# A fused two-layer gated block in fp32 on one core: key and value projections issued between the steps of the first attention, first transfers in another order, an additive mask table, weight signs in other slices

## The reference, cut to what matters

```python
x = x + tanh(g_xattn[0]) * L0_xattn(layernorm(x), ctx, mask_b)   # stage A, one head, keys = values = ctx
x = x + tanh(g_ffn[0])   * L0_ffn(layernorm(x), w1, w2, w3)      # stage B
x = x + tanh(g_xattn[1]) * L1_xattn(layernorm(x), ctx, mask_i, Wq, Wk, Wv, Wo, ...)  # stage C, 16 heads
x = x + tanh(g_ffn[1])   * L1_ffn(layernorm(x), w_gate, w_up, w_down)  # stage D
```

## Time and profile before

| | us |
|---|---|
| median of 3 executions | 259.05 |
| lowest, highest | 258.74, 261.1 |
| the profiled execution: its time | 261.3 |
| the profiled execution: its span | 259.5 |
| stage A, about | 11 to 40 |
| stage B, about | 40 to 127 |
| stage C, about | 127 to 184 |
| stage D, about | 184 to 259.5 |

### The profile page before, as it was taken

The page is one execution under the profiler, slowest core; times in us unless marked ns, Lnnn a source line. Parts: engine busy times, 40 slices in busy tenths (PEclk is TensorE's granted clock), DMA queues, the critical chain, the costliest instruction groups (busy, mean ns, idle before and its releaser), DMA issues. The chain is left out here.

```text
span 259.5 us, 5249 instructions
## 1 busy us (share of the span) xinstructions
PE 219.2 (84%) x1978; PEld 180.9 (70%) x1978; DVE 165.8 (64%) x449; ACT 139.8 (54%) x312; POOL 103.1 (40%) x143
## 2 busy tenths in 40 slices
PE   0285876859889889897889999997999999999992
PEld 0264634739769769776677787776888788888882
DVE  2769779778988988967615567779744424263333
ACT  1138785377757757758954677775323322222230
POOL 3501111156757757768522777777423000000000
PEclk9999555999999999999968999999999999999999
DMA  5999002900000000000000000000000000020002
GB/s 166 370 392 310 9 0 68 391 29 0 3 0 0 0 5 0 1 3 0 0 3 3 3 4 3 3 3 4 3 0 0 3 0 0 3 81 0 0 3 81
DMA packets 9240, 12.60 MB, mean 49 GB/s; under 512 B 1024, under 2 KB 7936, under 8 KB 9216
## 3 DMA queue, kind: packets, MB, share of 16 engines
q1 hardware_dynamic: 8784, 12.07, 13.4%
q10 hardware_dynamic: 432, 0.20, 0.4%
HBM read 11.22 MB, written 1.05 MB: 47 GB/s over the span
## 5 line engine op out<-in xcount | busy, mean ns | idle before, releaser
L1334 PE MATMUL PB<-SGN,WHI 128*128 128x512 f32 x128 | 40.6, 398 | 0.0
L725 DVE TENSOR_TENSOR WRAW<-WRAW,PB 128x512 f32<-128x512 f32 x16 | 11.0, 688 | 32.7 <-ACT WRAW L1037 32.7
L1037 ACT ACTIVATE WRAW<-PB 128x512 f32<-128x512 f32 x16 | 9.6, 597 | 34.8 <-PE PB L1334 34.8
L1119 PE MATMUL PB<-SGN,XQH 128*128 128x512 f32 x64 | 26.7, 417 | 1.3 <-DVE XQL L579 1.3
L1351 PE MATMUL PB<-WHI,SGN 128*128 128x256 f32 x128 | 25.6, 283 | 1.4 <-DVE SGN L733 1.4
L297 POOL TENSOR_TENSOR RSTD<-MVS,MHALF 128x1 f32<-128x1 f32 x24 | 14.4, 598 | 30.3 <-DVE MVS L427 30.2
L1119 PE MATMUL PB<-SGN,XQL 128*128 128x512 f32 x64 | 26.2, 409 | 0.0
L1334 PEld LDWEIGHTS PB<-SGN,WHI 128*128 128x128 f32 x128 | 23.0, 188 | 4.5
L1334 PE MATMUL PB<-SGN,WLO 128*128 128x512 f32 x64 | 25.4, 397 | 0.0
L332 POOL TENSOR_TENSOR HBQ<-HBQ,HR 128x512 f32<-128x512 f32 x16 | 17.5, 1096 | 15.7 <-DVE HR L616 15.7
L993 ACT ACTIVATE HBQ<-PB 128x512 f32<-128x512 f32 x32 | 17.5, 614 | 11.2 <-PE PB L1276 11.2
(11 more groups left out here) (129 smaller groups left out, 569.0 us busy)
## 6 DMA issues: line engine op xcount, KB each, us to landing
WRAW<-w_dram SPq DMA_DIRECT2D x2, 2048.0 KB, 12.0
X<-x_dram SPq DMA_DIRECT2D x2, 512.0 KB, 6.0
CTXT<-ctxt_dram SPq DMA_DIRECT2D x1, 1024.0 KB, 9.6
CTX<-ctx_dram SPq DMA_DIRECT2D x1, 1024.0 KB, 12.0
WRAW<-w_dram SPq DMA_DIRECT2D x1, 1024.0 KB, 14.9
WQK<-wqkvo_dram SPq DMA_DIRECT2D x1, 1024.0 KB, 7.7
WRAW<-wd_dram SPq DMA_DIRECT2D x1, 1024.0 KB, 10.0
out_dram<-X SPq DMA_DIRECT2D x4, 256.0 KB, 2.2
```

Of the source, the lines that this page charges most:

```text
L725: nc.vector.tensor_tensor(GU[:, b, :], SG[:, b, :], PB[2 * b + 1][:], ALU.mult).then_inc(d_g, 1)
L1119: mm = nc.tensor.matmul(PB[2 * half + m][:], part[:, p, c, :], sgn(m, c, a, b), start=(c == 0 and k == 0), stop=(c == DC - 1 and k == 1))
L1334: mm = nc.tensor.matmul(PB[2 * b + m][:], wcol(w_part, m, c, j), act_part[:, c, g * TG:(g + 1) * TG], start=(c == 0 and i == 0), stop=(c = ...
```

## The change

1. Key and value projections move from stage B to stage A. Instead of one call per context block in step t of stage B there are eight parts (KV_PARTS): four for keys, each with 2 matmuls of 512 columns, and four for values, each with 4 matmuls of 256 columns. PE issues part n at the end of step n + 1 of stage A, and the eighth after the loop; ACT copies each out one step later with one instruction of 512 columns. Key table KTA is now a tensor of its own.
2. First transfers: the key and value weights come right behind the context, then the small tables, then w0 in two halves, w3, and the other attention weights. ACT's own three small transfers are issued in the opposite order.
3. The mask is one additive table; the instruction at line 492 is gone. The table is made before the second half of the first statistics. The validity flags come out of it after step 0.
4. PE runs 14 matmuls on a table of ones before the first transposes.
5. Signs and absolute values: w0 in slices of 512 columns. No slices in steps 1 and 2, three sign slices in step 3, one sign and one absolute slice in each of steps 4 to 7. w3's signs and absolute values move behind stage A: signs in front of and behind the first silu, absolute values behind the second silu of step 0 of stage B.
6. The transfer of wd waits for w3's signs and absolute values. The scale of w3 gets a matmul and a DVE instruction of its own in step 1.

```diff
+WARMUPS = 14
+KV_PARTS = (("k", 0), ("k", 1), ("v", 0), ("k", 2), ("v", 1), ("k", 3), ("v", 2), ("v", 3))
+KV_AT = (1, 2, 3, 4, 5, 6, 7, 8)
...
             sp.wait_ge(w_sgn, NT)
-            sp.wait_ge(w_abs, NT)
+            sp.wait_ge(w_abs, 4)
             sp.wait_ge(w_abs1, NT)
             sp.dma_start(WRAW[:, 0:2, :].rearrange("p m (c n) -> p m c n", c=DC),
                          w1_in.rearrange("m c p n -> p m c n")).then_inc(ld["w1"], 16)
+            sp.wait_ge(w_sgn, NT + 2)
+            sp.wait_ge(w_abs, 6)
             sp.dma_start(WRAW[:, 2, :].rearrange("p (j n) -> p j n", j=FC),
                          wd_1.rearrange("j p n -> p j n")).then_inc(ld["wd"], 16)
...
                     nc.vector.scalar_tensor_tensor(
                         out=SM[:, p, :], in0=PB[2 + p][:, 0:P], scalar=1.0 / math.sqrt(D),
-                        in1=MASKF[:, t, :], op0=ALU.mult, op1=ALU.mult).then_inc(a_mk, 1)
+                        in1=MASKB[:, t, :], op0=ALU.mult, op1=ALU.add).then_inc(a_mk, 1)
...
+            def kv_out(n):
+
+                b, (what, i) = 4 + n % 2, KV_PARTS[n]
+                act.wait_ge(c_kv, n + 1)
+                if n == 0:
+                    act.wait_ge(ld["bias"], 16 * 8)
+                if what == "k":
+                    hc, g = i % DC, i // DC
+                    nc.scalar.activation(KTA[:, 4 * g:4 * g + 4, hc, :],
+                                         PB[b][:].rearrange("p (t n) -> p t n", t=4),
+                                         ACT.Identity, bias=BK[:, hc:hc + 1]).then_inc(c_kvo, 1)
+                else:
+                    nc.scalar.copy(VA[:, 2 * i:2 * i + 2, :],
+                                   PB[b][:].rearrange("p (t n) -> p t n", t=2)
+                                   ).then_inc(c_kvo, 1)
...
-                if t == 1:
+                if t == 3:
                     act.wait_ge(ld["w0"], 16)
-                if t == 2:
-                    act.wait_ge(ld["w3"], 16)
-                if live(t - 1):
+                    for k in range(3):
+                        sign_slice(k)
+                if t == 4:
+                    act.wait_ge(ld["w0b"], 16)
+                if t - 1 in KV_AT:
+                    kv_out(KV_AT.index(t - 1))
+                if t >= 4:
                     sign_slice(t - 1)
-                    abs_slice(t - 1)
+                    abs_slice(t - 4)
...
             pipeline(step_a, lag=0)
+            kv_out(6)
             sign_slice(NT - 1)
+            kv_out(7)
...
                     if t == 0:
+                        sign_w3(1)
                         hi_x(1, 1)
                     silu(t, 1)
+                if t == 0:
+                    abs_w3(0)
+                    abs_w3(1)
...
                 if live(t):
-                    kv_out(t)
                     hi_slice(t)
...
+            pe.wait_ge(set_pool, 2)
+            for _ in range(WARMUPS):
+                nc.tensor.matmul(PB[7][:, 0:P], ONES[:], ONES[:], start=True, stop=True)
             pe.wait_ge(ld["ident"], 16)
...
+                if t in KV_AT:
+                    kv(KV_AT.index(t))
...
-                if live(t):
-                    kv(t, p)
                 if live(t - 1):
                     down_b(t - 1, 0)
+            kv(7)
             pe.wait_ge(a_et, NT)
+            pe.wait_ge(c_kvo, 7)
             transpose_xq(0, 0)
```

More of the change, by code:

```diff
@@ L210, in head_at @@
             return j * 4 * P + (2 * c + e) * P
-        ld = {n: sem("ld_" + n) for n in ("x", "x2", "ctxt", "ctx", "mask", "small", "ident", "w0",
-                                          "w3", "qk", "bias", "w1", "wd")}
+        ld = {n: sem("ld_" + n) for n in ("x", "x2", "ctxt", "ctx", "mask", "small", "ident", "w0", "w0b",
+                                          "w3", "qk", "kv", "bias", "w1", "wd")}
         set_act, set_dve, set_pool = sem("set_act"), sem("set_dve"), sem("set_pool")
@@ L899, in hi_x @@
                                ).then_inc(b_xh, 1)
-            def kv_out(t):
-                act.wait_ge(c_kv, t + 1)
-                for c in range(DC):
-                    nc.scalar.activation(KTA[:, bass.ds(t, 1), c, :],
-                                         PB[5][:, c * P:(c + 1) * P].unsqueeze(1),
-                                         ACT.Identity, bias=BK[:, c:c + 1]).then_inc(c_kt, 1)
-                nc.scalar.copy(VA[:, bass.ds(t, 1), :], PB[5][:, D:2 * D].unsqueeze(1)
-                               ).then_inc(c_va, 1)
             def hi_slice(t):
@@ L1076, in scores_a @@
                 pe.wait_ge(a_ht, t + 1)
-                need(pe, a_mk, t - 1)
+                need(pe, a_et, t - 1)
                 for c in range(DC):
@@ L1098, in step_a, with kv @@
                                      start=True, stop=True).then_inc(a_ro, 1)
+                if t in KV_AT:
+                    kv(KV_AT.index(t))
+            def kv(n):
+                b, (what, i) = 4 + n % 2, KV_PARTS[n]
+                if n == 0:
+                    pe.wait_ge(ld["kv"], 16)
+                need(pe, c_kvo, n - 1)
+                if what == "k":
+                    hc, g = i % DC, i // DC
+                    for c in range(DC):
+                        mm = nc.tensor.matmul(PB[b][:], WQK[:, 1, c, hc * P:(hc + 1) * P],
+                                              CTXT[:, c, g * 512:(g + 1) * 512],
+                                              start=(c == 0), stop=(c == DC - 1))
+                else:
+                    for k in range(2):
+                        for c in range(DC):
+                            mm = nc.tensor.matmul(
+                                PB[b][:, k * D:(k + 1) * D],
+                                CTXT[:, c, (2 * i + k) * P:(2 * i + k + 1) * P],
+                                WQK[:, 2, c, :], start=(c == 0), stop=(c == DC - 1))
+                mm.then_inc(c_kv, 1)
             xt_a(0, 0)
@@ L1124, in down_b @@
             def down_b(u, k):
+                if u == 0 and k == 0:
+                    pe.wait_ge(w_sgn, NT + 2)
+                    pe.wait_ge(wsc3, 1)
                 if k == 0:
```

172 lines of the change are left out of this document (90 added, 82 removed).

## The result

| | before | after |
|---|---|---|
| median, same chip | 258.89 us (258.68 to 261.1) | 275.27 us (273.49 to 276.89) |
| ratio, 95% interval | | 1.0574 [1.0525, 1.0623] |
| profiled execution: time, span | 261.3, 259.5 us | 274.99, 273.2 us |

The kernel is 16 us slower. The forecast of 264.2 us had the sign right and a third of the size, and its range ended 6.8 us too early.

A forecast was written before the change was run, and what follows sets the result against it. ACT was taken to pace stage A, DVE stage B's loop; PE would pace A after the change. Terms 2.2 + 3.4 + 1.0 - 1.4 = +5.2 us on the median 259.05 gave 264.2 us, own range 261.7 to 268.5, wider range 258.5 to 268.5.

The forecast's parts named there:

- Projection in A, mask, start: Stage A up to the first silu of B: PE becomes its limit, warm-up wins some clock; +2.2 us, between +0.5 and +3.5.
- Stall for wd: Step 0 of B: wd's transfer, issued behind w3's absolute values, lands late and delays step 1's silu; +3.4 us, bounds 1.2 and 6.4.
- S: Start of the first silu of stage B; w3's absolute values were forecast to end at S + 5.1 us, wd to land at S + 9.5.
- Clock in the hole: While ACT stands waiting for wd, PE idles and the next gate_up runs at 1.2 GHz; +1.0 us, bounds 0 and 3.8.
- w3's scale: Steps 0 and 1 of B: one tiny matmul and two tiny DVE instructions, in the hole; 0, at most 0.3 us.
- Projection out of B: Seven steps of B, where DVE sets the loop, go from 9.66 to 9.47 us; -1.4 us, bounds 0 and -14.4.
- the clock falls in the steady steps of B: Rival: PE idles 2.6 of 9.5 us; every third step has gate_up at 1.2 GHz; +8, sum +13, 272 us; chance 0.10.
- Half the clock inside the steady steps: Sign of being wrong: half the clock in stage B's steady steps; no size given.
- C and D: Stages behind B, which the change leaves alone: as long as before, 0 us.
- the seam: Passage from stage A to B, up to the first silu of B; forecast +2.2 us.

The follow-up runs named there:

- scale earlier: The changed kernel, but DVE makes the scale of w3 behind the first product of step 1, not at that step's end: 269.02 us, ratio 1.0358 to before.

## Why the prediction was wrong

**Projection in A, mask, start: +2.2; measured +1.0.** Right within its range. Each of the six other kernels of this study that keep the projection in A had its first silu between 48.4 and 49.6, so the profiled 48.19 lies at the early end, and +1.9 is the mean of all seven. The step was forecast at 3.5 us and took 3.38, PE back to back; the mechanism held. But the sum hid two large terms: the rest of the change takes 5 to 6 us out of stage A and the projection puts 6 to 8 in. I had counted ACT's slices "2.0 us, as before" with the copy in them, without asking what they would be without it.

**Stall for wd: +3.4; step 0 measured +5.4.** The mechanism and the place were right, the sizes off: 4.4 to 4.7 us are the wait, 0.8 the clock. The line through the earlier trace rows gave 4.4 us for 1 MB; it took 5.6 (5.3 to 5.6 in the profiles of the kernels that issue it alone). The clock's part: the absolute values ended at S + 5.7 instead of 5.1, since the second silu first waited 1.07 us for a `gate_up` at 1.2 GHz. Of the Trainium skill's fit (DMA: Bandwidth & Descriptors, Anatomy of one DMA) I wrote that it is on the low side for 2 MB; it is for 1 MB too, 4.4 against 5.6. The page gives the fit for transfers that GpSimd issues; these were issued by SyncE.

**Clock in the hole: +1.0; w3's scale: 0, at most 0.3; together in step 1 measured +3.8.** Here a step of the working failed: "one tiny matmul and two tiny DVE instructions ... in the hole". I priced their durations and not the wait of `down_b` for them. The instruction in question is 0.21 us long; moving it alone brought 2.6 us ahead of `gate_up`. The clock's part, forecast at 1.0, was 1.25 by the same run. My own rule, to name for every added wait what is queued behind it, was applied to `hi_slice` and not to this one.

**Projection out of B: -1.4; measured +5.2.** This is the step that decided the error. That DVE sets the loop was right: with the clock up, a step takes 9.5 to 9.6 us without `kv`. The 0.2 us a step that I expected to gain did not come, since with `kv` and all else as changed it takes 9.6 too. And I took PE's work as something that can only cost. The rival *the clock falls in the steady steps of B* described what came, and I gave it 0.10 because the clock had stayed at 1.00 over 38 us "in spite of the gaps". That row was evidence for a PE that idles 1.0 us per step, not for one that idles 2.2. The rival's price, 8 us, was nearer to 5.2 than the forecast, and its 272 us to the result. That nearness is partly luck: it had every third step 3.8 us longer, and the runs showed five of six steps longer, by 0.9 to 1.6 us; it also held nothing for w3's scale. Half the clock inside the steady steps stood among my signs of being wrong, and it came.

The Trainium skill (TensorE: Matmul & The Clock Gate, HAM oscillation) ties the fall to idle gaps in a loop of matmuls and advises against long ones. Here no single gap in the steady steps was longer than 1.00 us, shorter than those that the section's rule speaks of, and the clock fell all the same. That more idling brings the fall agrees with this trace; that it takes a long gap does not, so the rule by its words spoke less for the rival than I wrote.

**C and D: 0; measured -1.6.** The kernel before had 5 us at half clock at the start of stage C in its profiled execution; the one after had not. The other profiles bear out that this stretch goes with the clock: it took 131.3 us in the kernel whose clock line has no low slice behind stage B (scale earlier) and 132.8 to 133.1 in those with one short low place there, the changed kernel among them. So I take the 134.6 as an accident of that one execution, which also stood 2.4 us above the median; the kernel before was profiled once.

Terms against the sum: 6.6 from the projection out of B, 2.0 from the stall, 2.8 from step 1 beyond the clock's 1.0, less 1.2 and 1.6 for the seam and C. But for rounding that is the 8.5 us between 13.7 and 5.2.

## What to carry to other kernels

Work that is taken out of a matmul engine's idle corner can cost time: in a loop that another engine sets, ask for what the granted clock will be with the larger gaps, and try the loop once with a few useless matmuls in their place. A tiny new instruction is priced by where its result is waited for and by whose PSUM bank it borrows. Two losses or gains of opposite sign in one stage hide in a sum that looks right; undoing one part at a time brings them out, and here it left a version 1.8% faster than the original.

## What the runs showed of the hardware

- Two extra matmuls of 256 columns per step of stage B, 1.03 us of PE, made a kernel 7 us faster (275.27 to 268.23); the granted clock stood at 1.00 through its steady steps of B, against 0.87 without them.
- The clock stayed at 1.00 for 38 us with 2.2 us of PE idling per step and then fell (mean 0.84 over the next 22 us) without any new wait. A quiet stretch at full clock is no proof that the pattern holds it.
- A transfer of 1 MB alone on the queue landed in 5.3 to 5.6 us; the same transfer issued right behind w1's 2 MB took 9.9 to 10.2 us, and w1's took 7.3 to 7.7 either way.
